# Two-layer adaptive-norm transformer block on one core: the last addition of x moved to GpSimd, ends of stages and the output projection rewritten

## The chip, the cores and the metric

The kernel runs on one core of one Trainium2 chip. The metric is device time in microseconds of one execution. Three executions of the kernel before took 2568.30, 2572.04 and 2572.55 us; the median is 2572.04 us. The execution that was profiled took 2576.07 us, and its profile spans 2574.3 us.

## The reference

`x` has 2 sequences of 2048 tokens, 256 wide, in float32. Both layers add a gated attention part and a gated feed-forward part. Cut to what matters:

```
mod = silu(c) @ wmod                      # sa, ca, ga, sb, cb, gb per sequence
h = layernorm(x)*(1+ca)+sa
x = x + ga * attention(h)                 # layer 0: 16 causal heads with rope; out @ W_o.T
h = layernorm(x)*(1+cb)+sb
x = x + gb * (h + expert[argmax(gate)](h))        # layer 0: top-1 of 8 experts, 256x256 each
h = layernorm(x)*(1+ca)+sa
x = x + ga * (silu-gated mix of 4 sequences(h) + h)   # layer 1
h = layernorm(x)*(1+cb)+sb
x = x + gb * (sum over the top 2 of 8 experts of w_e * FFN_e(rmsnorm(h)))
```

The output projection is `attention @ W_o.T`, and the last line's sum, gate and addition of `x` are the combination.

## The kernel before

The program is eight stages, one block of five instruction streams each: modulation, projections, attention, output projection, top-1 experts, layer 1 (mixing and routing), routed experts, combination. `k.x` (32 tiles of 128 tokens by 256) stays in SBUF throughout. Within a stage the engines are tied by semaphores alone, written out by hand; there is no scheduler. Each stage ends with a barrier of the five engines. At it every engine runs a DRAIN, GpSimd (POOL) too, and then waits for the others. Between blocks SyncE (SP) clears the semaphores of the stage that ended, one instruction each (line 2326 in `end_stage`), and only then comes to its own part of the next block; the other engines don't wait for the clearing.

GpSimd issues direct DMAs in modulation and attention and indirect ones (scatters) in layer 1 and the routed experts. In the other stages it has only arithmetic, or nothing.

Output projection: for each of 8 chunks of 512 tokens ScalarE copies `k.x` to `still`, TensorE turns it with 8 transposes into `p_t`, ScalarE copies that to `aT`, TensorE makes 8 products of 256 columns into `p_o`, VectorE multiplies by the gate (line 1036), adds the input (line 1040) and takes row statistics (line 250). `still`, `aT`, `p_t` and `p_o` have one buffer each. TensorE waits for the weights before its first transposes.

Top-1 experts: SP loads the expert weights at the stage's start. ScalarE rounds them (lines 1154, 1156), GpSimd subtracts to get the low parts (lines 1129, 1132), and ScalarE comes to the first tile's `hT` (line 1140) after its rounding. In layer 1 VectorE waits, before it centers its first rows, for the routing tables, the last of SP's twelve loads, to copy the token numbers (line 1829). At that stage's end SP writes zeros behind the last row of each expert, ten DMAs, eight of them with an address read from SBUF (lines 1395 and 1398).

Combination: for each of 8 chunks ScalarE scales the first expert's rows (line 2263), VectorE adds the second's (line 2272, four instructions), multiplies by the gate (line 2275) and adds `k.x` (line 2277); SP stores each chunk.

## Time and profile before

| | |
|---|---|
| median of 3 executions | 2572.04 us (2568.30 to 2572.55) |
| the profiled execution | 2576.07 us |
| its span | 2574.3 us |
| TensorE busy (matmul) | 2215.2 us (86%) |
| VectorE busy | 1698.4 us (66%) |
| ScalarE busy | 1275.8 us (50%) |
| GpSimd busy | 871.4 us (34%) |
| mean granted TensorE clock | 0.926 |

Shares of busy time are means over eight stages with different limits. An end of a stage is a point that all engines pass, so a microsecond gained before one is gained by all that follows, unless what follows waits for something else. Such ends are read from the timeline, and from the instructions recorded at the block's own line (its DRAINs and semaphore instructions).

### The profile page before, as it was taken

The page shows a single profiled execution, that of the slowest core. Times are in us where ns is not written, and L with a number is a line of the kernel's source. Part 1 is how long each engine was busy: PE and PEld are TensorE (multiplying, and loading weights), DVE is VectorE, ACT ScalarE, POOL GpSimd, SP SyncE. Part 2 cuts the span into 40 slices and gives each one's busy share as a digit, 9 for nine tenths or more (in the row PEclk, how much of TensorE's full clock was granted, in tenths as well). Part 3 has the DMA queues.
Part 4 walks back from the last instruction along what each step waited for, and adds up shares of the span by engine and source line. Part 5 has one row for each costly group of instructions (what it writes and reads, how often), then busy time and mean ns, then how long its engine had stood idle before and what let it go on. Part 6 is the DMA issues. An engine that isn't in the chain of part 4 may idle for free. (4 is left out here: it accounts for less than half of the span.)

```text
span 2574.3 us, 39299 instructions
## 1 busy us (share of the span) xinstructions
PE 2215.2 (86%) x12968; PEld 1404.0 (55%) x12968; DVE 1698.4 (66%) x2697; ACT 1275.8 (50%) x2451; POOL 871.4 (34%) x1055
## 2 busy tenths in 40 slices
PE   3886999999999999986799779972899999999991
PEld 1673233333333333325577546642788888888880
DVE  4784878778777878844688668863455555555555
ACT  1231477666767767773223244421455555555452
POOL 3344223221230311200655422444344434444340
PEclk8896799999999999998899889985999999999995
DMA  4359503150413400002000100013453433444326
GB/s 169 98 156 182 88 2 47 23 68 2 67 15 55 48 21 3 2 1 70 33 0 0 32 1 1 33 38 139 144 173 130 149 128 128 161 160 138 126 73 206
DMA packets 126575, 200.16 MB, mean 78 GB/s; under 512 B 13696, under 2 KB 98688, under 8 KB 124992
## 3 DMA queue, kind: packets, MB, share of 16 engines
q1 hardware_dynamic: 109696, 141.45, 16.6%
q0 software_dynamic: 15600, 52.25, 10.7%
q10 hardware_dynamic: 1104, 4.20, 1.2%
q8 instruction: 102, 1.67, 0.3%
q14 instruction: 73, 0.60, 0.1%
HBM read 150.97 MB, written 46.88 MB: 77 GB/s over the span
## 5 line engine op out<-in xcount | busy, mean ns | idle before, releaser
L905 DVE TENSOR_REDUCE tile_max<-p_m 128x2 f32<-128x1024 f32 (+3 forms) x640 | 651.4, 1060 | 150.1 <-PE p_m L767 78.7
L867 ACT ACTIVATE probs<-p_s 128x512 f32<-128x512 f32 (+3 forms) x1280 | 597.3, 534 | 247.9 <-PE p_s L776 243.0
L2061 PE MATMUL p_up<-f_xT,f_w 128*128 128x512 f32 (+1 forms) x2304 | 463.2, 350 | 8.2 <-POOL f_w L2224 8.2
L2061 PEld LDWEIGHTS p_up<-f_xT,f_w 128*128 128x128 f32 x2304 | 368.3, 189 | 58.8 <-issue 8.6
L714 POOL TENSOR_SCALAR_AFFINE_SELECT probs<-probs 128x128 f32<-128x128 f32 x512 | 145.7, 294 | 724.2 <-ACT probs L867 715.5
L763 PE MATMUL p_m<-ka,qa 96*128 96x512 bf16 (+3 forms) x1280 | 363.9, 367 | 29.5 <-PEq L330 17.4
L776 PE MATMUL p_s<-qa,ka 99*128 99x512 bf16 (+3 forms) x1280 | 353.8, 353 | 19.6 <-DMA qa<-max_scr 8.3
L2224 POOL TENSOR_TENSOR f_w<-f_raw,f_w 128x1024 fp32r<-128x1024 f32 x96 | 231.6, 2416 | 408.0 <-ACT f_w L2113 408.0
L790 PE MATMUL p_o<-probs,va 128*32 128x512 f32 (+3 forms) x2560 | 302.4, 544 | 0.3 <-POOL probs L714 0.3
L2076 PE MATMUL p_y<-f_w,f_hidden 128*128 128x256 f32 x1872 | 256.3, 283 | 28.9 <-DVE f_hidden L2178 14.6
L2076 PEld LDWEIGHTS p_y<-f_w,f_hidden 128*128 128x128 f32 x1872 | 237.7, 188 | 50.9 <-issue 31.7
L763 PEld LDWEIGHTS p_m<-ka,qa 96*128 96x128 bf16 x1280 | 111.7, 100 | 261.2 <-DVE tile_max L905 140.2
L2174 DVE SCALAR_TENSOR_TENSOR f_gate<-p_up,f_b,f_gate 128x512 f32<-128x512 f32 (+1 forms) x192 | 124.6, 649 | 194.0 <-ACT f_gate L2126 187.7
L776 PEld LDWEIGHTS p_s<-qa,ka 99*128 99x128 bf16 x1280 | 111.2, 98 | 228.3 <-ACT probs L867 139.7
L2178 DVE TENSOR_TENSOR f_hidden<-f_gate,f_hidden 128x512 fp32r<-128x512 f32 (+1 forms) x192 | 133.9, 698 | 118.7 <-ACT f_hidden L2131 114.0
L2126 ACT ACTIVATE f_gate<-p_up,f_b 128x512 f32<-128x512 f32 (+1 forms) x192 | 116.4, 606 | 172.2 <-PE p_up L2061 159.9
L1173 PE MATMUL p_e<-w_expert,c_hT 128*128 128x512 f32 x768 | 196.6, 406 | 0.0
L2131 ACT ACTIVATE f_hidden<-f_gate 128x512 fp32r<-128x512 f32 (+1 forms) x192 | 105.9, 552 | 159.5 <-DVE f_gate L2174 138.5
L1173 PEld LDWEIGHTS p_e<-w_expert,c_hT 128*128 128x128 f32 x768 | 141.4, 191 | 29.9
L2113 ACT ACTIVATE f_w<-f_raw 128x1024 fp32r<-128x1024 f32 x144 | 150.4, 1045 | 5.4 <-DMA f_raw<-in_W1b 3.6
L507 PE MATMUL p_qk<-hT,wqkv 128*128 128x512 f32 x384 | 99.3, 418 | 18.1 <-DVE rot L406 15.7
L1591 PE MATMUL p_uv<-l_xnT,w_uv 128*128 128x512 f32 x256 | 112.9, 598 | 0.0
(251 smaller groups left out, 2579.5 us busy)
## 6 DMA issues: line engine op xcount, KB each, us to landing
f_raw<-in_W1a SPq DMA_DIRECT2D x24, 1024.0 KB, 6.1
f_raw<-in_W1b SPq DMA_DIRECT2D x24, 1024.0 KB, 8.5
f_raw<-in_W SPq DMA_DIRECT2D x24, 1024.0 KB, 11.2
qk_scr<-parts SPq DMA_DIRECT2D x48, 256.0 KB, 2.5
qa<-qk_scr POOLq DMA_DIRECT2D x42, 256.0 KB, 15.4
ka<-qk_scr POOLq DMA_DIRECT2D x42, 256.0 KB, 17.2
v_scr<-wqkv_raw SPq DMA_DIRECT2D x32, 256.0 KB, 3.3
g_ys<-y_rows SPq DMA_DIRECT2D x16, 512.0 KB, 8.8
```

The lines of the kernel that those rows point to most:

```text
L714: last = nc.gpsimd.affine_select(block_, block_, pattern=[[1, P]], compare_op=ALU.is_ge, fill=0.0, base=0, channel_multiplier=-1)
L763: last = nc.tensor.matmul(p_m[:, at_bank, hh, 0:width], qa[buf][0:QROWS, hd, q0:q0 + P], ka[buf][0:QROWS, hd, bank * CH:bank * CH + width] ...
L776: nc.tensor.matmul(p_s[:, s_bank(x, buf), lo:CH], ka[buf][0:QROWS + SPLIT, h, j * P:(j + 1) * P], qa[buf][0:QROWS + SPLIT, h, c * CH + lo: ...
L790: last = nc.tensor.matmul(p_o[VW * h:VW * (h + 1), lo:CH], va[buf][:, j, VW * h:VW * (h + 1)], probs[:, (buf * UNITS + n) % NPROBS, h, lo: ...
L867: nc.scalar.activation(probs[:, (buf * UNITS + n) % NPROBS, h, lo:CH], p_s[:, s_bank(("exp", HG * n + h), buf), lo:CH], ACT.Exp, scale=DH ...
L905: nc.vector.tensor_reduce(out=tile_max[:, 2 * hp:2 * hp + 2, i, bank], in_=p_m[:, at_bank, :, 0:width], op=ALU.max, axis=AX.X).then_inc(ma ...
L1173: last = nc.tensor.matmul(out, hT[:, par, hp, kt, :], weights(wp, kt), start=(kt, wp, hp) == (0, HI, HI), stop=(kt, wp, hp) == (KT - 1, LO ...
L2061: last = nc.tensor.matmul(p_up[:, f % 2, ab, 0:size], w1[:, wh, ab * KT + kt, f * P:(f + 1) * P], xT[:, t % 2, xh, kt, 0:size], start=(kt, ...
L2076: last = nc.tensor.matmul(p_y[:, u, :], hidden[:, f % 2, hh, u * P:(u + 1) * P], w2[:, wh, f, :], start=(f, wh, hh) == (0, HI, HI) and u % ...
L2113: nc.scalar.activation(piece_part(q, HI), piece_raw(q, par), ACT.Copy).then_inc(w_high, 1)
L2178: nc.vector.tensor_tensor(hidden[:, f % 2, LO, 0:size], gate[:, f % 2, 0:size], hidden[:, f % 2, HI, 0:size], ALU.subtract).then_inc(hidde ...
L2224: nc.gpsimd.tensor_tensor(piece_part(q, LO), piece_raw(q, t % 2), piece_part(q, HI), ALU.subtract).then_inc(w1_ready, 1)
```

## The change

Six things change; attention's and the routed experts' inner loops, the projections and the steady part of the top-1 experts stay.

1. In the combination GpSimd adds `k.x` instead of VectorE.
2. Attention, layer 1 and the routed experts end without GpSimd's DRAIN.
3. SP clears the semaphores of the stage before after it has issued its first loads (in attention, before its first transfer).
4. The output projection is unrolled and has two buffers of `still`, `aT`, `p_t` and `p_o`. TensorE turns chunk i+1 before the products of chunk i, and turns chunk 0 before it waits for the weights.
5. The expert weights of the next stage are loaded, rounded (ScalarE) and subtracted (GpSimd) in the output projection.
6. In layer 1 the token numbers are copied when the first group chooses; and ScalarE's queue takes five of the ten zero writes.

```diff
-        with nc.Block() as block:                        # attention, layer 1, routed experts
+        with nc.Block(no_gpsimd_drain=True) as block:
...
 def output_projection(nc, a, k, ew):
             def _(sp):
                 sp.dma_start(w[:, :, :], a["woT"]...).then_inc(w_loaded, 16)
                 load(0)
                 load(1)
+                sp.dma_start(ew.raw_gate[:, :, :], ...).then_inc(e_loaded, 16)
+                sp.dma_start(ew.iota[:, :], a["iota8"]).then_inc(e_loaded, 16)
+                sp.dma_start(ew.raw[:, :, :], a["expertT"]...).then_inc(e_loaded, 16)
+                clear_last_stage(sp)
...
+            def _(pool):
+                pool.wait_ge(e_high, 1)
+                nc.gpsimd.tensor_tensor(ew.gate[:, LO, :, :], ew.raw_gate[:, :, :], ew.gate[:, HI, :, :],
+                                        ALU.subtract).then_inc(e_ready, 1)
+                for bank in range(BANKS):
+                    pool.wait_ge(e_high, bank + 2)
+                    nc.gpsimd.tensor_tensor(ew.bank(ew.w[:, LO, :, :], bank), ew.bank(ew.raw, bank), ew.bank(ew.w[:, HI, :, :], bank),
+                                            ALU.subtract).then_inc(e_ready, 1)
+                pool.wait_ge(e_ready, 1 + BANKS)
...
+                keep(0)                                  # ScalarE: keep copies k.x, copy takes p_t
+                keep(1)
+                for i in range(NCH):
+                    copy(i)
+                    if i + 2 < NCH:
+                        keep(i + 2)
+                    if i == NCH - BANKS - 1:
+                        act.wait_ge(e_loaded, 16 * E_LOADS)
+                        nc.scalar.activation(ew.gate[:, HI, :, :], ew.raw_gate[:, :, :], ACT.Copy).then_inc(e_high, 1)
+                    if NCH - BANKS - 1 <= i < NCH - 1:
+                        round_bank(i - (NCH - BANKS - 1))
...
+                turn(0)                                  # TensorE
+                pe.wait_ge(w_loaded, 16)
+                for i in range(NCH):
+                    if i + 1 < NCH:
+                        turn(i + 1)
                     pe.wait_ge(aT_ready, i + 1)
-                    if not first(i):
-                        pe.wait_ge(scaled, i)
+                    if i >= 2:
+                        pe.wait_ge(scaled, i - 1)
...
 def top1_experts(nc, a, k, ew):
-                act.wait_ge(loaded, 16 * LOADS)
-                nc.scalar.activation(gate[:, HI, :, :], raw_gate[:, :, :], ACT.Copy).then_inc(w_high, 1)
-                for bank in range(BANKS):
-                    nc.scalar.activation(bank_of(w, HI, bank), raw[:, :, bank * CH:(bank + 1) * CH], ACT.Copy).then_inc(w_high, 1)
                 round_hT(0, 0)
...
 def layer1(nc, a, k):
+                zero_tails(sp, range(E1 // 2), 0)
+                zero_tails(act, range(E1 // 2, E1), 1)
                     if g == 0:
                         dve.wait_ge(route_loaded, 16 * ROUTE_LOADS)
+                        c_own.add(nc.vector.tensor_copy(row_ids[:, :, 0], token_no))
...
-                dve.wait_ge(route_loaded, 16 * ROUTE_LOADS)
-                c_own.add(nc.vector.tensor_copy(row_ids[:, :, 0], token_no))
                 dve.wait_ge(rstd_all, 1)
...
 def combine(nc, a, k, out):
+                clear_last_stage(sp)                     # after the 16 loads
...
+            @block.gpsimd
+            def _(pool):
+                for i in range(NCH):
+                    pool.wait_ge(gated, i + 1)
+                    nc.gpsimd.tensor_tensor(res[:, rows_of(i), :], res[:, rows_of(i), :], k.x[:, rows_of(i), :], ALU.add).then_inc(done, 1)
...
                     nc.vector.tensor_tensor(rows, rows, k.mod(1, i // CPS, GB), ALU.mult).then_inc(gated, 1)
-                    dve.wait_ge(gated, i + 1)
-                    nc.vector.tensor_tensor(rows, rows, k.x[:, rows_of(i), :], ALU.add).then_inc(done, 1)
...
 def end_stage(nc):
-    for sem in Mem.of_stage:
-        nc.sync.sem_clear(sem)
+def clear_last_stage(sp):
+    for sem in Mem.cleared:
+        sp.sem_clear(sem)
```

TensorE at the end of attention and the start of the output projection, before (`o_pt` and `o_po` are the PSUM tiles of the transposes and of the products):

```order
L806 MATMUL p_m<-ident,o_sb 128x128 x3
L698 UNCONDITIONAL_BRANCH
L1007 UNCONDITIONAL_BRANCH [waits barrier_Pool_Activation_PE_DVE_SP_release]
L1013 MATMUL o_pt<-ident,o_still 128x128 [waits o_still_ready,o_w_loaded]
L1013 MATMUL o_pt<-ident,o_still 128x128 x7
L1021 MATMUL o_po<-wo,o_aT 128x256 [waits o_aT_ready]
L1021 MATMUL o_po<-wo,o_aT 128x256 x7
```

The same place after:

```order
L808 MATMUL p_m<-ident,o_sb 128x128 x3
L699 UNCONDITIONAL_BRANCH
L1059 UNCONDITIONAL_BRANCH [waits barrier_Pool_Activation_PE_DVE_SP_release]
L1067 MATMUL o_pt<-ident,o_still 128x128 [waits o_still_ready]
L1067 MATMUL o_pt<-ident,o_still 128x128 x7
L1067 MATMUL o_pt<-ident,o_still 128x128 [waits o_still_ready,o_w_loaded]
L1067 MATMUL o_pt<-ident,o_still 128x128 x7
L1081 MATMUL o_po<-wo,o_aT 128x256 [waits o_aT_ready]
L1081 MATMUL o_po<-wo,o_aT 128x256 x7
```

A second set of transposes now stands ahead of the first products, and the wait for the weights (`o_w_loaded`) stands one chunk later.

SP at the end of the routed experts and in the combination, before (`f_b` is a bias, `g_ys` the experts' rows, `g_res` the result; line 2326 is the clearing):

```order
L2032 DMA f_b<-in_b 128x256
L2007 UNCONDITIONAL_BRANCH
L2326 ISA [waits barrier_Pool_Activation_PE_DVE_SP_release]
L2326 ISA x22
L2245 UNCONDITIONAL_BRANCH
L2250 DMA g_ys<-y_rows 128x4x256 x16
```

and after (line 2370 is the clearing):

```order
L2063 DMA f_b<-in_b 128x256
L2038 UNCONDITIONAL_BRANCH
L2277 UNCONDITIONAL_BRANCH [waits barrier_Pool_Activation_PE_DVE_SP_release]
L2282 DMA g_ys<-y_rows 128x4x256 x16
L2370 ISA x23
```

The 23 clears moved from ahead of the 16 loads to behind them.

GpSimd from the end of attention to the first steps of the top-1 experts, before (`probs` belongs to attention, `c_h` to the first tiles of the top-1 experts):

```order
L714 AFFINE_SELECT probs<-probs 128x128 [waits probs_ready] x160
L698 UNCONDITIONAL_BRANCH
L1100 UNCONDITIONAL_BRANCH [waits barrier_Pool_Activation_PE_DVE_SP_gather]
L260 TENSOR_TENSOR rstd<-ve,neghalf 128x32 [waits ve_ready]
L1105 TENSOR_TENSOR c_h<-c_h,mods 128x256 [waits c_h_centered]
```

and after:

```order
L715 AFFINE_SELECT probs<-probs 128x128 [waits probs_ready] x160
L699 UNCONDITIONAL_BRANCH
L1020 UNCONDITIONAL_BRANCH [waits barrier_Pool_Activation_PE_DVE_SP_gather]
L1023 TENSOR_TENSOR w_gate<-c_raw_gate,w_gate 128x16 [waits o_e_high]
L1027 TENSOR_TENSOR w_expert<-c_raw,w_expert 128x2x512 [waits o_e_high] x4
L1001 UNCONDITIONAL_BRANCH [waits o_e_ready]
```

The five subtractions of the expert weights moved into the output projection, where GpSimd had nothing.

## Rows read from the trace of the kernel before

**Rows 1.** End of attention on VectorE, and the start of the output projection (timeline).

```profile
start us, us, engine line op out<-in xcount [idle before <-releaser]
1165.58 0.42 DVE L933 TENSOR_TENSOR x<-p_m,recip 128x256 f32<-128x256 f32 x1
1171.05 1.06 ACT L997 ACTIVATE o_still<-x 128x1024 f32<-128x1024 f32 x1 [6.65 <-PEq L698]
1172.09 0.43 SPq L984 DMA_DIRECT2D wo<-in_woT  x1
1174.99 1.97 PE L1013 MATMUL o_pt<-ident,o_still 128*128 128x128 f32 x8 [9.81 <-DMA wo<-in_woT]
1178.07 4.27 PE L1021 MATMUL o_po<-wo,o_aT 128*128 128x256 f32 x12 [1.11 <-ACT o_aT L1001]
```

**Rows 2.** GpSimd's DRAINs at three stage ends (ns min/median/max, start us).

```profile
L698 POOLq DRAIN  x1: 7972/7972/7972, 1162.8 to 1162.8; - x1
L1376 POOLq DRAIN  x1: 5382/5382/5382, 1782.6 to 1782.6; - x1
L2007 POOLq DRAIN  x1: 6417/6417/6417, 2523.8 to 2523.8; - x1
```

**Rows 3.** A steady chunk of the output projection, and its last statistics (timeline).

```profile
1196.61 3.32 PEld L1021 LDWEIGHTS o_po<-wo,o_aT 128*128 128x128 f32 x16 [1.35 <-ACT o_aT L1001]
1199.96 1.01 PEld L1013 LDWEIGHTS o_pt<-ident,o_still 128*128 128x128 f32 x8
1226.21 1.40 DVE L250 BATCH_NORM_STATS2 stats<-x  x4
```

**Rows 4.** Start of the top-1 experts (timeline).

```profile
1236.76 0.69 PE L1167 MATMUL c_pt<-ident,c_h 128*128 128x128 f32 x2 [13.60 <-POOL c_h L1107]
1241.28 0.36 ACT L1140 ACTIVATE c_hT<-c_pt 128x256 fp32r<-128x256 f32 x1
```

**Rows 5.** Start of layer 1 (timeline).

```profile
1468.54 5.44 POOL L1434 TENSOR_TENSOR rstd<-ve,neghalf 128x32 f32<-128x32 f32 x1 [3.31 <-DVE ve L243]
1479.42 0.20 DVE L1829 COPY xn_rows<-r_table 128x32 f32<-128x32 f32 x1 [10.94 <-DMA r_table<-in_tile_table]
```

**Rows 6.** End of layer 1, start of the routed experts (timeline).

```profile
1769.62 17.11 SPq L1398 DMA_DIRECT2D x_slots<-u_sb  x10
1785.38 0.41 DVE L1946 COPY weights<-r_pair_weights 128x16 f32<-128x16 f32 x4
1793.84 0.41 SPq L2016 DMA_DIRECT2D f_x<-x_slots  x1
```

**Rows 7.** SP's clears after layer 1 (instructions of a line, ns); combination's loads (timeline).

```profile
L2326 SPq EVENT_SEMAPHORE_RANGE_CLEAR  x42: 25/30/40, 1790.2 to 1793.0; - x42
...
2531.83 19.60 SPq L2250 DMA_DIRECT2D g_ys<-y_rows  x16
```

**Rows 8.** The combination: a load-paced ScalarE step, first and last VectorE work (timeline).

```profile
2540.59 1.71 ACT L2263 ACTIVATE g_res<-g_ys,weights 128x256 f32<-128x256 f32 x4 [1.31 <-DMA g_ys<-y_rows]
2538.12 1.68 DVE L2272 SCALAR_TENSOR_TENSOR g_res<-g_ys,weights,g_res 128x256 f32<-128x256 f32 x4 [19.60 <-ACT g_res L2263]
2569.80 1.23 DVE L2277 TENSOR_TENSOR g_res<-g_res,x 128x1024 f32<-128x1024 f32 x1
```

**Rows 9.** VectorE beside GpSimd's 128x1024 additions in layer 1 (timeline).

```profile
1490.57 3.39 DVE L1684 TENSOR_SCALAR l_h<-x,mean,rstd 128x256 f32<-128x256 f32 x4
1498.44 1.38 DVE L1684 TENSOR_SCALAR l_h<-x,mean,rstd 128x256 f32<-128x256 f32 x4
1644.69 4.65 POOL L1412 TENSOR_TENSOR l_h<-l_h,l_ob 128x1024 f32<-128x1024 f32 x2
1644.78 4.66 DVE L1673 TENSOR_TENSOR r_same<-l_logits,r_best 128x64 f32<-128x64 f32 x1
```

**Rows 10.** GpSimd's DMA issues by line: ns min/median/max, first and last start.

```profile
L281 POOL DMA_DIRECT2D ka<-qk_scr x42: 505/505/539, 234.4 to 880.3; - x42
L1429 POOL DMA_INDIRECT x_slots<-xn_rows,slots x64: 956/962/6556, 1613.8 to 1778.9; - x64
L2216 POOL DMA_INDIRECT y_rows<-f_y,f_y_to x78: 954/967/986, 1861.7 to 2520.5; - x78
```

More of the change, by code:

```diff
@@ L976, in output_projection, with rows_of @@
         scaled, x1_ready = m.sem("o_scaled"), m.sem("o_x1_ready")
+        e_loaded, e_high, e_ready = m.sem("o_e_loaded"), m.sem("o_e_high"), m.sem("o_e_ready")
+        E_LOADS = 3
+        def rows_of(i):
+            return slice(i * TPC, (i + 1) * TPC)
         with nc.Block() as block:
@@ L986, in _ @@
-                load(1, 1)
-                with sp.Fori(1, NCH // 2) as i:
-                    for par in range(2):
-                        sp.wait_ge(x1_ready, 2 * i + par - 1)
-                        load(2 * i + par, par)
+                load(0)
+                load(1)
+                sp.dma_start(ew.raw_gate[:, :, :], a["gateT"].rearrange("(k p) n -> p k n", p=P)).then_inc(e_loaded, 16)
+                sp.dma_start(ew.iota[:, :], a["iota8"]).then_inc(e_loaded, 16)
+                sp.dma_start(ew.raw[:, :, :], a["expertT"].rearrange("(k p) n -> p k n", p=P)).then_inc(e_loaded, 16)
@@ new lines, in _ @@
+                clear_last_stage(sp)
+                for i in range(2, NCH):
+                    sp.wait_ge(x1_ready, i - 1)
+                    load(i)
+                sp.wait_ge(e_loaded, 16 * E_LOADS)
+            @block.gpsimd
[8 more added lines that the diff above has]
+                pool.wait_ge(e_ready, 1 + BANKS)
@@ L1003, in _, with keep, copy @@
-                chunk(0)
-                with act.Fori(1, NCH) as i:
-                    chunk(i)
+                def keep(i):
+                    if i >= 2:
+                        act.wait_ge(turned, i - 1)
+                    nc.scalar.activation(still[:, i % 2, :, :], k.x[:, rows_of(i), :], ACT.Copy).then_inc(still_ready, 1)
+                def copy(i):
+                    act.wait_ge(turned, i + 1)
+                    if i >= 2:
+                        act.wait_ge(product, i - 1)
+                    nc.scalar.activation(aT[:, i % 2, :, :], p_t[:, i % 2, :, :], ACT.Copy).then_inc(aT_ready, 1)
@@ L1007, in _, with turn @@
             @block.tensor
             def _(pe):
-                def chunk(i):
+                def turn(i):
                     pe.wait_ge(still_ready, i + 1)
+                    if i >= 2:
+                        pe.wait_ge(aT_ready, i - 1)
                     for kt in range(KT):
                         for u in range(TPC):
-                            last = nc.tensor.transpose(p_t[:, kt, u * P:(u + 1) * P], still[:, u, kt * P:(kt + 1) * P],
+                            last = nc.tensor.transpose(p_t[:, i % 2, kt, u * P:(u + 1) * P], still[:, i % 2, u, kt * P:(kt + 1) * P],
@@ L1374, in p_logits, with zero_tails @@
             return p_l_last if j == 2 * LAST + 1 else p_l[:, j % 2, :, :]
-        with nc.Block() as block:
+        def zero_tails(engine, experts, part):
+            engine.wait_ge(tails_ready, 1)
+            engine.dma_start(k.x_slots[E1 * REGION + part * HT:E1 * REGION + (part + 1) * HT, :].rearrange("(p u) d -> p (u d)", p=P),
+                             zeros).then_inc(tails_zeroed, 16)
+            for e in experts:
+                at_row = engine.value_load(k.tails[0:1, e:e + 1], min_val=0, max_val=NSLOT - ST)
+                engine.dma_start(k.x_slots[bass.ds(at_row, HT), :].rearrange("(p u) d -> p (u d)", p=P), zeros).then_inc(tails_zeroed, 16)
+        with nc.Block(no_gpsimd_drain=True) as block:
             @block.sync
@@ L2005, in last_tile @@
             return t == NTILES - 1
-        with nc.Block() as block:
+        with nc.Block(no_gpsimd_drain=True) as block:
             @block.sync
@@ L2256, in _ @@
                 sp.wait_ge(stored, 16 * NCH)
+            @block.gpsimd
+            def _(pool):
+                for i in range(NCH):
+                    pool.wait_ge(gated, i + 1)
+                    nc.gpsimd.tensor_tensor(res[:, rows_of(i), :], res[:, rows_of(i), :], k.x[:, rows_of(i), :], ALU.add).then_inc(done, 1)
             @block.scalar
```

112 lines of the change are left out of this document (43 added, 69 removed).

## The prediction

> **What bounds the kernel now.** I read the page first. TensorE is busy 86% of the span, but the slices in which it falls to 0 to 7 tenths are the ends of stages and the last slice, and those are where the change acts. So I read, in order, the instructions recorded at each block's own line (who came last to each barrier), the timeline on both sides of each barrier, a steady chunk of the output projection, and the combination. The reader is to see five places where nothing useful happens, and one engine that sets the pace at the end.
>
> At the end of attention VectorE finishes at 1165.58 + 0.42 = 1166.0 us [rows 1], but ScalarE starts the next stage at 1171.05. The last to arrive is GpSimd: its DRAIN runs from 1162.8 for 7.97 us, to 1170.77 [rows 2]; passing the barrier takes the other 0.28 us. After the routed experts it is the same: a DRAIN of 6.42 us from 2523.8, then SP's clears, and the first load at 2531.83 [rows 2, 7]. After layer 1 a DRAIN of 5.38 us ends at 1788.0, but SP is later still: its ten zero writes take 17.11 us to issue, it passes the barrier just ahead of its first clear at 1790.2, clears until 1793.0 and issues the first load at 1793.84, while VectorE was done at 1785.79 [rows 2, 6, 7]. In the output projection a chunk is a chain in one buffer: the weights' loads of the products run from 1196.61 to 1199.96 and those of the transposes 1.01 us more, then TensorE waits 1.35 us for ScalarE's copy [rows 3]. In the combination ScalarE waits for each load (1.71 us of work and 1.31 of waiting, 3.02 per chunk [rows 8]), and VectorE, from 2538.12 to 2571.03, takes 32.9 us for 8 chunks, 4.11 each [rows 8]: VectorE is the bound there, the loads would be the next.
>
> **The change part by part**, against the profiled execution (2576.07 us, span 2574.3).
>
> *End of attention.* Without the DRAIN the barrier opens at 1166.0 + 0.28 = 1166.3. ScalarE's copy ends at 1167.3, the transposes and the second copy take what they took, 1178.07 - 1174.99 = 3.08 us [rows 1]; the second set of transposes stands ahead of the products and adds up to 1 us, so the products start at 1171.3. The weights are issued at 1166.4 and landed 2.90 us after their issue before (1172.09 to 1174.99 [rows 1]), so at 1169.3: not late. Before, the products started at 1178.07: -6.8 us.
>
> *Two buffers.* Before, from 1178.07 to the last statistics at 1227.61 [rows 1, 3]: 49.5 us. After, TensorE needs 3.35 + 1.05 = 4.40 us a chunk with no wait. VectorE needs three operations of 1.23, 1.23 and 1.40 us [rows 3, 8] and small gaps, some 3.95, and stays below that. First chunk 5 us (the slow one, [rows 1]: 4.27 for 12 of its 16 products), seven of 4.40, then 0.6 and 3.95 for VectorE: 40.3. That is -9.2 us. GpSimd's four new subtractions can hold VectorE's addition (below); most of that goes into VectorE's slack of 0.45 us a chunk, and I take +0.5 back. ScalarE has three operations of about 1.05 us a chunk in 4.40 and hides the rounding. Range of this part -6 to -10.
>
> *Start of the top-1 experts.* The transposes end at 1237.45, but ScalarE comes to their result at 1241.28 because it rounds weights until then [rows 4]. The rounding is gone: -3.8 us. What is late next is the chain through `rstd` and the transposes, which is already in that 1237.45.
>
> *Start of layer 1.* `rstd` is there at 1468.54 + 5.44 = 1473.98, yet VectorE stands until 1479.42 for the routing tables [rows 5]. The wait goes, a copy of 0.2 us comes back later: -5.3 us.
>
> *End of layer 1.* SP's tail is split in two queues, so that either issues five of ten writes in about half of 17.11 us, from 1769.6 to some 1778, and VectorE, done at 1785.79 [rows 6], becomes the last. Barrier at 1786.1, then the 0.84 us that SP took from its last clear to the first load (1793.0 to 1793.84 [rows 6, 7]): 1786.9 against 1793.84, -6.9 us. The 42 clears now stand after the loads of the second tile, where SP waits for its turn anyway.
>
> *End of the routed experts.* Barrier at 2523.8 + 0.3 and no clears ahead of the loads: 2524.1 against 2531.83, -7.7 us.
>
> The sum up to here: 6.8 + 8.7 + 3.8 + 5.3 + 6.9 + 7.7 = 39.2 us earlier.
>
> *GpSimd's addition in the combination.* VectorE loses 1.23 us of work a chunk, GpSimd gets an addition of 4.65 / 2 = 2.3 us by the layer 1 pair [rows 9], 2.4 taken. It would fit beside VectorE if the two ran side by side. In layer 1 they don't: a VectorE operation on 64 elements per row lasted 4.66 us because it started 0.09 us after the first of two such additions, and ended with the second [rows 9], and four others that take 1.38 us took 3.39 beside the pair's first [rows 9]. So one addition costs VectorE 3.39 - 1.38 = 2.0 to about 2.3 us. All that VectorE still does in the combination has both inputs in SBUF, like the first of these. I take 2.2. Then: 8 x 2.86 of VectorE's own, seven additions in its way at 2.2, the last with nothing beside it, 0.1 + 2.4: 22.9 + 15.4 + 2.5 = 40.8 us against 32.9, +7.9 (by 2.0 and 2.4: +6.5 and +9.3). The part that was moved to relieve VectorE makes its stage longer.
>
> The Trainium skill says more (SBUF — State Buffer, Who interferes with whom): a VectorE instruction with two SBUF inputs and a GpSimd instruction that reads SBUF share a read interface, and the second to issue blocks until the first is finished. By that rule every addition costs its whole length, seven times 2.4, and the stage is at the upper of my two values; these rows agree within 0.4 us an addition. It is the rule that speaks against moving work from the one engine to the other here.
>
> *Where the DRAINs go.* The one of attention took 7.97 us although its last DMA had been issued at 880.3 to 881 us, some 280 us before, and 160 GpSimd operations of attention lay between [rows 2, 10]. So it does not wait for transfers, and arithmetic on GpSimd does not work it off. Its length follows the number of DMAs since the last DRAIN: 5.38 us for 64, 6.42 for 78 [rows 2, 10], 0.084 and 0.082 us each. Leaving the instruction out then only defers the cost to the next DRAIN. For attention's that is the output projection's, which GpSimd reaches with its last subtraction, about chunk 6, some 12 us ahead of the stage's end: hidden, worth +0 (up to 8 if it were reached last). For layer 1's 64 and the routed experts' 78 it is the combination's, after the last addition: 142 x 0.083 = 11.8 us, where before only 2574.3 - 2571.03 = 3.3 us lay between the last addition and the end, the store. So +8.5 us. No trace shows a deferred DRAIN; the ends are 0 (it costs nothing if put off) and 8.5, and I take 8.5, since the attention row is just that case: late, and paid in full.
>
> Sum: -39.2 + 7.9 + 8.5 = -22.8 us; 2576.07 becomes 2553.3. The profiled execution lies 4.0 us over the median of the runs shown, 2572.04, so I predict 2549 for the median.
>
> **The rivals.**
> - *The DRAIN's cost isn't carried over*, or only the last stage's 78 DMAs (6.4 instead of 11.8, +3.1 over the store). For it: nothing shows two stages' DMAs in one DRAIN. Against it: attention's row. The time: 2549.2 - 8.5 = 2540.7, or 2543.8.
> - *The barriers don't open earlier*: the flag leaves the waiting somewhere else, in the next GpSimd instruction or in the barrier itself. Then attention gives back 4.8 us (1170.77 - 1166.0), layer 1 2.2 (1788.0 - 1785.8), the routed experts 6.4, and the combination's 8.5 doesn't arise: 2549.2 + 13.4 - 8.5 = 2554. Little speaks for it, since each engine's barrier step waits only for the others' signal.
> - *GpSimd adds beside VectorE*. Then the combination is paced by the loads: 7 x 3.02 + 2.9 + 2.4 = 26.4 us instead of 32.9, and the time is 2549.2 - 7.9 - 6.5 = 2535. Against it: all of rows 9.
> - *Slower than before: the scatters pay.* With no DRAIN since the output projection, GpSimd might have to clean up its finished DMAs inside the routed experts, at each scatter. A tile lasts (2523.8 - 1793.84) / 24 = 30.4 us; GpSimd works 4 x 2.3 for the subtractions and 3.25 scatters of 1.27 us (0.97 and a gap of 0.3) in it, which leaves 17 us, 5.2 for each scatter. Up to there it is hidden. If each scatter paid a whole DRAIN, 6.4 us, the stage would grow by 78 x 1.2 = 95 us, to some 2644 us; it turns into a loss over 0.2% from 0.36 us beyond the 5.2. Against it: 78 scatters stay within 954 and 986 ns, and attention's many direct DMAs within 505 and 539, with no clean-up in any [rows 10].
>
> **How the numbers follow.** The forecast 0.55, no or partial carrying 0.22, barriers unchanged 0.08, additions side by side 0.05, slower 0.04; the remaining 0.06 is for gains at stage starts that the next stage swallows (2555 to 2566). The likeliest case's own range, from the bounds of the addition's price and of the output projection, is 2544 to 2555. The range that should hold 8 in 10 reaches down to the uncarried DRAIN and up past the unchanged barriers: 2538 to 2558. A change below 0.2% (5.1 us) can't be told from none here. Every case but the last is faster by more than that: faster 0.94, same 0.02, slower 0.04.
>
> **What would show it.** In the profile after: ScalarE starts the output projection within 0.5 us of attention's last VectorE work; products begin there every 4.4 us; layer 1's first centering follows `rstd` at once; SP's first load of the routed experts comes about 1.1 us after VectorE's last copy. In the combination VectorE's four `g_res` operations that follow an addition take about 3.9 us instead of 1.7, a chunk lasts 5.1 us, and the last row of all is a GpSimd DRAIN near 11.8 us. I am wrong if that DRAIN is short, if the chunk lasts near 3 us, or if the subtractions in the output projection hold VectorE so that its chunks take over 5 us.

## The result, and the profile after

Four executions of the changed kernel took 2537.22 to 2539.70 us, median 2538.45; four of the kernel before, on the same chip, 2568.30 to 2572.55, median 2571.53 (the three shown first and one of 2571.02). The ratio is 0.9873, 95% interval 0.9856 to 0.9891. The forecast was 2549 with a range of 2538 to 2558: the time lies in the range, half a microsecond from its lower end, and outside the 2544 to 2555 of the likeliest case. From the median of 2572.04 it is 33.6 us, where 23.0 were forecast.

The profiled execution took 2537.22 us and spans 2535.5 us, 38.8 less than before. The barriers that end the stages, read in every profile from GpSimd's semaphore step at the block's line, give the length of each stage. The experiments stand beside for use below; every row is one profiled execution.

| us | to the end of projections | attention | output projection | top-1 | layer 1 | routed | combination |
|---|---|---|---|---|---|---|---|
| before | 232.8 | 938.1 | 56.9 | 239.4 | 322.8 | 740.4 | 43.8 |
| after | 232.2 | 929.9 | 42.4 | 235.1 | 311.1 | 731.2 | 53.5 |
| addition on VectorE | 230.9 | 930.7 | 42.9 | 235.3 | 311.2 | 731.7 | 42.6 |
| no last DRAIN | 232.0 | 930.5 | 43.0 | 235.5 | 311.2 | 731.8 | 50.1 |
| DRAIN after routed | 231.1 | 930.3 | 43.2 | 235.5 | 311.6 | 737.9 | 50.0 |
| before + GpSimd's addition | 232.0 | 932.9 | 56.8 | 239.6 | 322.4 | 739.8 | 51.2 |
| parts in PSUM | 232.4 | 933.5 | 42.3 | 235.1 | 310.1 | 732.1 | 38.1 |
| one buffer | 232.4 | 934.0 | 54.8 | 234.9 | 309.8 | 729.7 | 53.3 |
| clears first | 234.0 | 932.4 | 44.5 | 235.5 | 310.1 | 733.3 | 54.5 |
| zeros on SP | 232.8 | 935.8 | 42.9 | 235.4 | 311.0 | 732.1 | 53.2 |
| DRAINs back | 232.5 | 938.0 | 43.5 | 237.1 | 314.7 | 737.6 | 49.5 |
| longer chain | 232.4 | 935.8 | 43.0 | 235.4 | 310.8 | 738.3 | 50.1 |
| one new DMA | 232.3 | 931.0 | 43.1 | 235.6 | 311.3 | 731.5 | 53.0 |

End of attention and start of the output projection after, in the timeline (columns as in [rows 1], to which they answer).

```profile
1161.45 0.42 DVE L935 TENSOR_TENSOR x<-p_m,recip 128x256 f32<-128x256 f32 x1
1162.25 0.43 SPq L1008 DMA_DIRECT2D wo<-in_woT  x1
1162.26 2.00 ACT L1036 ACTIVATE o_still<-x 128x1024 f32<-128x1024 f32 x2 [1.98 <-PEq L699]
...
1163.37 3.62 PE L1067 MATMUL o_pt<-ident,o_still 128*128 128x128 f32 x16 [2.31 <-ACT o_still L1036]
...
1166.57 3.48 PEld L1081 LDWEIGHTS o_po<-wo,o_aT 128*128 128x128 f32 x16
...
1202.95 1.41 DVE L250 BATCH_NORM_STATS2 stats<-x 128x6 f32<-128x256 f32 x4
```

ScalarE starts 0.4 us behind VectorE's last work, where it was 5.05. Products start 4.70 us behind it, where it was 12.07, and from there to the last statistics it is 37.8 us, where it was 49.5 [rows 1, 3]. But VectorE itself is done 4.1 us sooner than before, in a stage whose loop the change doesn't touch. Two stretches of that loop, before and then after (busy time and count of PE, PEld, DVE, ACT, POOL; granted clock; DMA share; GB/s):

```profile
560.00:600.00 40.00, 37.99 (x244) 13.65 (x242) 26.86 (x36) 26.27 (x55) 4.56 (x16) 0.91 0.23 43
```

```profile
560.00:600.00 40.00, 39.19 (x269) 14.59 (x269) 30.67 (x41) 28.91 (x60) 4.54 (x16) 1.00 0.18 38
```

In this stretch TensorE was for a while at 1.2 instead of 2.4 GHz in the one execution and not in the other (a mean granted clock of 0.91 and of 1.00), and got 244 instead of 269 multiplications done. Such dips come in every profile here, most at changing places; attention without a DRAIN behind it lasts 929.9 to 935.8 us in the table. Added up in stretches of 20 us from 240 to 1140, the time that the clock withheld (one less the granted clock, times 20) is 35.4 us before and 31.8 after; it is 30.4 in the kernel with a DRAIN after the routed experts, whose attention lasts 930.3, and 37.4 in the one with all zero writes on SP, where it lasts 935.8. So 3.6 of the 4.1 us are the clock's dips and not a gain; the execution profiled before lay 4.0 us over its median.

GpSimd's DRAINs after (ns min/median/max, start), which answer to [rows 2]:

```profile
L1001 POOLq DRAIN  x1: 7492/7492/7492, 1193.3 to 1193.3; - x1
...
L2276 POOLq DRAIN  x1: 8829/8829/8829, 2526.4 to 2526.4; - x1
...
L2276 SPq DRAIN  x1: 7/7/7, 2531.9 to 2531.9; - x1
```

Attention's DRAIN is paid in the output projection, 7.49 us, and ends at 1200.8, ahead of VectorE: hidden. The last DRAIN starts while the last addition runs (below) and outlasts it by 6.4 us; SP had its stores landed at 2531.8, so 3.4 us of it are on the path, not 8.5. Here one of the prediction's own signs fails: the DRAIN is not near 11.8 us.

A chunk of the output projection beside a subtraction of the expert weights, the first steps of top-1 and of layer 1 ([rows 3, 4, 5]):

```profile
1178.79 2.37 POOL L1027 TENSOR_TENSOR w_expert<-c_raw,w_expert 128x1024 fp32r<-128x1024 f32 x1 [0.71 <-ACT w_expert L1045]
...
1179.15 1.22 DVE L1089 TENSOR_TENSOR o_gated<-o_po,mods 128x1024 f32<-128x1024 f32 x1 [0.34 <-PE o_po L1081]
1179.71 3.32 PEld L1081 LDWEIGHTS o_po<-wo,o_aT 128*128 128x128 f32 x16
...
1180.48 1.76 DVE L1093 TENSOR_TENSOR x<-o_gated,o_xin 128x1024 f32<-128x1024 f32 x1
...
1184.04 3.32 PEld L1081 LDWEIGHTS o_po<-wo,o_aT 128*128 128x128 f32 x16
...
1213.49 0.69 PE L1195 MATMUL c_pt<-ident,c_h 128*128 128x128 f32 x2 [13.61 <-POOL c_h L1147]
1214.22 0.38 ACT L1172 ACTIVATE c_hT<-c_pt 128x256 fp32r<-128x256 f32 x1 [20.18 <-PE c_pt L1195]
...
1440.92 5.44 POOL L1465 TENSOR_TENSOR rstd<-ve,neghalf 128x32 f32<-128x32 f32 x1 [3.31 <-DVE ve L243]
...
1446.40 1.38 DVE L1716 TENSOR_SCALAR l_h<-x,mean,rstd 128x256 f32<-128x256 f32 x4 [5.53 <-POOL rstd L1465]
```

Products come every 4.33 us. VectorE's addition, both inputs in SBUF, is held until the subtraction ends (1.76 for 1.23 us); its multiplication, which reads PSUM, is not, although it lies wholly beside the subtraction. ScalarE and VectorE start the next two stages as soon as their inputs are there.

The end of layer 1 and the combination ([rows 6, 7, 8]), and with them who came last to layer 1's barrier (ns min/median/max, first and last start):

```profile
1745.45 0.96 POOL L1460 DMA_INDIRECT x_slots<-xn_rows,slots  x1 [0.30 <-issue]
...
1747.60 0.40 DVE L1977 COPY weights<-r_pair_weights 128x16 f32<-128x16 f32 x4
1751.55 0.42 SPq L2047 DMA_DIRECT2D f_x<-x_slots  x1
...
L1412 DVEq DRAIN  x1: 431/431/431, 1747.6 to 1747.6; - x1
L1412 SPq DRAIN  x1: 7/7/7, 1748.7 to 1748.7; - x1
L1412 POOLq EVENT_SEMAPHORE  x2: 17/17/17, 1750.6 to 1750.7; - x2
...
2482.03 19.85 SPq L2282 DMA_DIRECT2D g_ys<-y_rows  x16
...
2488.75 1.68 DVE L2311 SCALAR_TENSOR_TENSOR g_res<-g_ys,weights,g_res 128x256 f32<-128x256 f32 x4 [12.25 <-ACT g_res L2302]
...
2496.76 3.75 DVE L2311 SCALAR_TENSOR_TENSOR g_res<-g_ys,weights,g_res 128x256 f32<-128x256 f32 x4
2496.92 2.52 POOL L2295 TENSOR_TENSOR g_res<-g_res,x 128x1024 f32<-128x1024 f32 x1 [2.81 <-DVE g_res L2314]
...
2526.47 2.34 POOL L2295 TENSOR_TENSOR g_res<-g_res,x 128x1024 f32<-128x1024 f32 x1 [2.41 <-DVE g_res L2314]
```

VectorE is done at 1748.0, but SP's first load of the routed experts comes 3.55 us later and not 1.1: a second sign that fails. The last at the barrier is GpSimd, also without its DRAIN: its last scatter is issued at 1746.4, and it waits until 1750.6 for its scatters to land (a semaphore wait in the kernel).

VectorE's four `g_res` operations take 3.75 us beside an addition, 1.68 alone. From its first work to the end of the last addition it is 40.06 us, where it was 32.9.

### The profile page after: what moved, and what is told of

Read it like the earlier page. It is cut to its first block and busy times, and to the rows that moved or that the text cites. A ratio compares the mean times of both kernels' runs of the same rounds, so it can differ in the third digit from the quotient of the medians.

```text
span 2535.5 us, 39140 instructions
## 1 busy us (share of the span) xinstructions
PE 2208.5 (87%) x12968; PEld 1402.7 (55%) x12968; DVE 1703.5 (67%) x2689; ACT 1274.9 (50%) x2451; POOL 889.7 (35%) x1063
## 3 DMA queue, kind: packets, MB, share of 16 engines
q0 software_dynamic: 15600, 52.25, 10.9%
## 5 line engine op out<-in xcount | busy, mean ns | idle before, releaser
L869 ACT ACTIVATE probs<-p_s 128x512 f32<-128x512 f32 (+3 forms) x1280 | 597.0, 535 | 244.4 <-PE p_s L778 239.6
L765 PE MATMUL p_m<-ka,qa 96*128 96x512 bf16 (+3 forms) x1280 | 363.8, 367 | 29.1 <-PEq L330 17.2
```

The source lines that it names most:

```text
L765: last = nc.tensor.matmul(p_m[:, at_bank, hh, 0:width], qa[buf][0:QROWS, hd, q0:q0 + P], ka[buf][0:QROWS, hd, bank * CH:bank * CH + width] ...
L869: nc.scalar.activation(probs[:, (buf * UNITS + n) % NPROBS, h, lo:CH], p_s[:, s_bank(("exp", HG * n + h), buf), lo:CH], ACT.Exp, scale=DH ...
```

## The experiments

The spread of a kernel's executions is some ±4 us, as large as single terms, so where a term is small it is read from its stage in the table, and the median stands beside. The ratios are to the kernel before on the same chip, whose median was 2571.36 to 2573.70 us on the three chips that ran the experiments.

No run takes back the move of the expert weights (part 5) or of the token numbers (part 6). Their worth stands on the rows shown above.

**The addition back on VectorE.**

```diff
-            @block.gpsimd                            # combination: its additions
                     nc.vector.tensor_tensor(rows, rows, k.mod(1, i // CPS, GB), ALU.mult).then_inc(gated, 1)
+                    dve.wait_ge(gated, i + 1)
+                    nc.vector.tensor_tensor(rows, rows, k.x[:, rows_of(i), :], ALU.add).then_inc(done, 1)
```

> The changed kernel with one part undone: the last addition of x in the combination is VectorE's again, GpSimd has nothing to do there. Theory (while GpSimd adds, it holds VectorE's four additions of g_res: 3.75 us for four instead of about 1.7; the DRAIN at the program's end belongs to the scatters of the routed experts): a chunk of the combination takes 4.1 us instead of 4.93, the stage from VectorE's first to its last work 32.9 us instead of 40.1, and GpSimd's DRAIN stands at the stage's start, 6.4 us long, hidden. The span ends 42.5 us (43.9 less 1.4 of clears) after the barrier at 2482.0: 2524.5 against 2535.5, so about 11 us less than the changed kernel, median near 2527.5, ratio to before 0.983. Rival 1 (the four additions last 3.75 us for another reason, such as the loads): chunk stays at 4.9 us plus VectorE's own addition or is unchanged, time 2535 or more. Rival 2 (the DRAIN covers layer 1's 64 scatters too): its length is 8.8 (if it ran beside the last addition in the changed kernel) or 11.8 us.

Measured: median 2529.86 us (five, 2527.08 to 2533.14), ratio 0.9842 (0.9829 to 0.9856); the stage 42.6 instead of 53.5 us. VectorE's rows in the timeline, and the DRAIN's:

```profile
2501.42 1.67 DVE L2305 SCALAR_TENSOR_TENSOR g_res<-g_ys,weights,g_res 128x256 f32<-128x256 f32 x4
2503.12 1.22 DVE L2308 TENSOR_TENSOR g_res<-g_res,mods 128x1024 f32<-128x1024 f32 x1
2504.38 1.22 DVE L2310 TENSOR_TENSOR g_res<-g_res,x 128x1024 f32<-128x1024 f32 x1
2505.53 1.67 DVE L2305 SCALAR_TENSOR_TENSOR g_res<-g_ys,weights,g_res 128x256 f32<-128x256 f32 x4
```

```profile
L2276 POOLq DRAIN  x1: 6431/6431/6431, 2482.8 to 2482.8; - x1
```

The chunk is 4.11 us again, and with nothing ahead of it the DRAIN is 6.43 us: that of 78 scatters, not of 142. The theory holds, both rivals fall. By the stage, the addition on GpSimd costs the change 10.9 us: 7.1 by holding VectorE, 3.4 by the DRAIN that it pushes to the end, the rest between the first load and the first work. By the medians it is 8.6.

**The kernel before, with that addition alone.** The diff is the reverse of the one above, in the kernel before.

> The kernel before, with only the combination's last addition of x moved to GpSimd. Theory (each addition holds VectorE about 2.0 us and saves it 1.23): chunk 4.9 instead of 4.11 us, four g_res additions 3.75 us, stage 7 us longer, and no DRAIN of length at the end, since the one after the routed experts has done its work (0.05 us there): median 2571.5 + 7.2 = 2578.7, ratio 1.003. Rival (the two engines work side by side when loads come as in the kernel before, and the changed kernel's longer stage comes from its clears or its DRAIN): chunk 3.0 to 4.1 us, median 2565 to 2571.

Measured: median 2580.39 us (eight), ratio 1.0034 (1.0024 to 1.0044); the stage 51.2 instead of 43.8 us. The addition makes its stage 7.4 us longer by itself, against 7.2 expected; the medians differ by 9.0. This profile is also a second one of the old end of layer 1, and there it differs from [rows 6]:

```profile
1763.47 9.99 SPq L1398 DMA_DIRECT2D x_slots<-u_sb  x10
...
1774.62 0.41 DVE L1946 COPY weights<-r_pair_weights 128x16 f32<-128x16 f32 x4
...
1787.45 0.41 SPq L2016 DMA_DIRECT2D f_x<-x_slots  x1
```

```profile
L1376 POOLq DRAIN  x1: 5382/5382/5382, 1778.2 to 1778.2; - x1
```

The ten writes take 10.0 us, not 17.1. The barrier waits for GpSimd's DRAIN (to 1783.6), not for SP.

**No DRAIN at the end.**

```diff
-        with nc.Block() as block:                    # combination
+        with nc.Block(no_gpsimd_drain=True) as block:
```

> The changed kernel, and the combination too ends without GpSimd's DRAIN. Theory (the last DRAIN of 8.83 us, 6.4 of it behind the last addition, stands on the path by 3.4 us over the store): no DRAIN at the end, the span ends about 3.4 us sooner, at 2532, median near 2535. Rival (whatever was put off is paid at the end of the program in any case, in another instruction or in the time after the span): median 2538 as in the changed kernel.

Measured: median 2535.13 us (four, 2529.82 to 2539.95), ratio 0.9855 (0.9837 to 0.9874); the stage 50.1 instead of 53.5 us, -3.4 as expected. The executions of the two kernels overlap, so the medians alone (3.3 us apart) would not show it; but the stage is 53.0 to 53.5 us in the four profiles that end with this DRAIN of 8.8 us and have their clears behind the loads, and 50.1 here. Nor is it paid behind the span: from the span to the device time it is 1.7 us in both.

**A DRAIN after the routed experts.** That block's flag is taken away, attention's and layer 1's stay.

> The changed kernel with GpSimd's DRAIN at the end of the routed experts restored, while attention and layer 1 stay without it. Theory A (a DRAIN deals only with the DMAs of the stage that ends): 6.4 us there for 78 scatters, as in the kernel before, and the DRAIN at the program's end is 2.4 us (the last addition alone). Theory B (what layer 1's DRAIN would have done is carried over, 0.083 us for each of 142): 11.8 us. Theory C (142 carried at a lower price, 8.8 us in all as in the changed kernel's last DRAIN): 8.8 us. The boundary costs its DRAIN in full and the program's end gives 3.4 us back, so against the changed kernel: A +3.0, B +8.4, C +5.4 us.

Measured: median 2540.81 us, ratio 0.9881 (0.9866 to 0.9896). The two DRAINs:

```profile
L2038 POOLq DRAIN  x1: 6439/6439/6439, 2483.0 to 2483.0; - x1
```

```profile
L2276 POOLq DRAIN  x1: 2447/2447/2447, 2533.9 to 2533.9; - x1
```

Theory A: what layer 1's DRAIN would have done is not in it (2.45 us at the end is the last addition alone). The stage grows by 6.7 us and the last gives 3.5 back, +3.2 against +3.0 expected.

**A longer chain without a DRAIN.** The flag in attention, the output projection, top-1 and layer 1, and a DRAIN after the routed experts.

> The changed kernel with GpSimd's DRAIN left out in attention, the output projection, the top-1 experts and layer 1, and restored after the routed experts: nothing cleans up between attention's 91 DMAs, layer 1's 64 and the routed experts' 78. Theory Own (a DRAIN deals with the DMAs of the last stage that had any): 6.4 us after the routed experts. Theory Sum (all of them): 233 x 0.082 = 19.2 us. Theory Pair (attention's part survives because it was carried over a stage before): 6.4 + 7.5 = 13.9 us. If Own holds, the question is where attention's 7.5 us were paid: in an instruction of layer 1, or never.

Measured, one execution: 2547.65 us (clock dips in attention, 935.8 us). The DRAIN:

```profile
L2038 POOLq DRAIN  x1: 6435/6435/6435, 2489.2 to 2489.2; - x1
```

This is what Own expected. Nor were attention's 7.5 us paid elsewhere: layer 1 and the routed experts last 310.8 and 738.3 us, 311.6 and 737.9 in the run before, where attention's DRAIN had been paid. In layer 1 one scatter, the thirtieth, takes 6.56 us, but it does so in every kernel, also behind DRAINs, and the smallest, the middle and the largest of the 64 are the same (956, 962, 6561 ns; [rows 10]: 956, 962, 6556).

**One new DMA behind attention's.**

```diff
-                sp.dma_start(ew.iota[:, :], a["iota8"]).then_inc(e_loaded, 16)
...
+                pool.dma_start(ew.iota[:, :], a["iota8"]).then_inc(i_loaded, 16)     # first on GpSimd
```

> The changed kernel, with the small load of iota_e in the output projection issued by GpSimd instead of SP, at the stage's start. So attention's 91 DMAs, whose DRAIN was left out, are followed by one new DMA before the next DRAIN. Theory Stage (a DRAIN deals only with the DMAs issued since the stage before ended): the output projection's DRAIN is 0.1 us. Theory Debt (what was put off stays until a DRAIN, whatever comes between): 7.6 us. Theory Last-N (the DRAIN's length follows a number of the newest DMAs that stays constant or is bounded): 7.5 us. The stage is hidden either way, no change in time expected.

Measured, one execution: 2539.66 us. The output projection's DRAIN:

```profile
L1002 POOLq DRAIN  x1: 7565/7565/7565, 1195.2 to 1195.2; - x1
```

One new DMA doesn't wipe out what was put off (7.57 against 7.49 us), so Stage falls, and with it Own's wording: the last stage that had any DMA is here the output projection, with one. Debt fits here, but 6.4 us after 233 DMAs above is against it, and against Last-N too, which couldn't be shorter there than here.

**All three DRAINs back.**

> The changed kernel with GpSimd's DRAIN restored at the ends of attention, layer 1 and the routed experts. Theory (each was on the path in full once SP's clears and zero writes are out of the way, and the last stage's is deferred to the end where 3.4 us of it show): attention's boundary +4.7 us, layer 1's +5.4, the routed experts' +6.4, the program's end -3.4: +13 us, median 2551.5. Rival (the prediction's reading of layer 1, where SP and VectorE are the last and the DRAIN is worth 2.2 us at most): layer 1's stage grows by 2 to 3 us only, +10 us.

Measured: median 2555.65 us (four, 2548.74 to 2556.69), ratio 0.9932 (0.9911 to 0.9953). By stage: attention's barrier 4.8 us behind VectorE instead of 0.2, +4.6; layer 1 +3.6; routed experts +6.4; combination -4.0. That is +10.6 and nearer the rival's 10 than the theory's 13, since layer 1 grew by less than its DRAIN's 5.3. The median is 17.2 us higher. What the other 6.6 are is not shown; in the profile attention is 3.5 us longer up to VectorE's end, the output projection 1.1 and top-1 2.0.

**One buffer.** `i % 2` becomes 0 in the four tiles, and the waits are for the chunk before.

```diff
-                turn(0)
...
-                    if i + 1 < NCH:
-                        turn(i + 1)
+                    turn(i)
...
                     pe.wait_ge(aT_ready, i + 1)
-                    if i >= 2:
-                        pe.wait_ge(scaled, i - 1)
+                    if i >= 1:
+                        pe.wait_ge(scaled, i)
```

> The changed kernel with one buffer each of o_still, o_aT, o_pt and o_po in the output projection (the kernel before's chain of keep, transposes, copy, products; the weights are still waited for behind the first transposes, and the expert weights' rounding stays here). Theory (the two buffers bring most of the stage's gain): chunk 5.7 us instead of 4.33, the span from the first product to the last statistics 47.5 instead of 37.8 us, median 2538.5 + 10 = 2548.5. Rival (most of the stage's gain is that TensorE's clock is back at full speed sooner, or that the input loads come earlier): chunk below 5 us, median under 2543.

Measured: median 2551.11 us (four), ratio 0.9907 (0.9889 to 0.9925); the stage 54.8 instead of 42.4 us. The first two chunks, and the clock there and in the changed kernel:

```profile
1170.77 5.94 PEld L1075 LDWEIGHTS o_po<-wo,o_aT 128*128 128x128 f32 x16 [1.58 <-issue]
...
1179.09 3.32 PEld L1075 LDWEIGHTS o_po<-wo,o_aT 128*128 128x128 f32 x16 [1.35 <-ACT o_aT L1042]
...
1184.80 3.32 PEld L1075 LDWEIGHTS o_po<-wo,o_aT 128*128 128x128 f32 x16 [1.35 <-ACT o_aT L1042]
```

```profile
1171.00:1175.00 4.00, 4.00 (x10) 3.16 (x11) 0.00 (x0) 0.60 (x1) 0.00 (x0) 0.50 1.07 399
```

```profile
1167.00:1171.00 4.00, 4.00 (x23) 3.54 (x23) 0.51 (x1) 2.14 (x3) 0.00 (x0) 1.00 1.07 363
```

A chunk is 5.71 us instead of 4.33: 7 x 1.38 = 9.7 us. The other 2.5 us are the first chunk's: with one set of transposes and a wait ahead of the products, TensorE does them at 1.2 GHz (0.50) and takes 5.94 us; with two sets and no pause it is at 2.4 GHz by then and takes 3.48. The theory's 10 us are there, and the rival's clock adds 2.5 to them; that the clock is most of the gain, as the rival had it, is false.

**Clears ahead of the stages.** `end_stage` clears again, `clear_last_stage` does nothing.

> The changed kernel with SP's clears of the last stage's semaphores ahead of each stage again. Theory (each clear costs SP 0.067 us and the first loads wait for them where nothing else is late): the routed experts' first load comes 2.8 us later (42 clears), the combination's first load 1.5 us later (23), and the output projection's wo about 1 us later, hidden behind the first transposes and copy; median 2538.5 + 4.3 = 2542.8. Rival (other work hides the clears everywhere): no change, 2538.5.

Measured: median 2545.87 us (four), ratio 0.9885 (0.9867 to 0.9902). By stage: output projection +2.1, top-1 +0.4, layer 1 -1.0, routed experts +2.1, combination +1.0, 4.6 in all, against 4.3 expected. The median is 7.4 us higher, of which 2.2 are this chip's (the kernel before took 2573.70 on it). The size by stage was right, the place was not: I had called `wo` hidden, but issued 1.2 us behind the barrier (1167.57) instead of 0.1 it holds up the second transposes, whose queue place is behind the wait for it, and TensorE comes to the first products at a lower clock (4.23 instead of 3.48 us).

**Ten zero writes on SP.**

> The changed kernel with all ten zero writes at the end of layer 1 in SP's queue, as before. Theory N (the 17.1 us that they took in the profile of before belong to that one execution: in another profile of the same code they took 9.7 us, from 1763.5 to 1773.2, and VectorE's tail 12.9 instead of 17.6 us): they are issued within 10 us of 1735.3, GpSimd stays the last at the barrier, no change, median 2538.5 within 1. Theory P (the prediction's reading: ten in one queue take 17.1 us): SP is last, at 1752.4 and the landing of 4 us more, the barrier opens at 1757 instead of 1750.7, median 2544.

Measured: median 2540.74 us (four, 2534.99 to 2545.08), ratio 0.9862 (0.9844 to 0.9880); layer 1 311.0 us, as with two queues.

```profile
1743.84 8.90 SPq L1432 DMA_DIRECT2D x_slots<-u_sb  x8
1752.78 1.09 SPq L1434 DMA_DIRECT2D x_slots<-u_sb  x2
```

This is what theory N expected: the ten take 10.0 us, and the median is the changed kernel's but for the 2.2 us of this chip. SP, with its writes landed, comes to the barrier at 1757.7, GpSimd at 1757.9, so one queue is just fast enough. Splitting the writes brought nothing here; 17.11 us was one execution's.

**Parts in PSUM.** The unheld multiplication in the output projection suggested it.

```diff
+        part = m.ps("g_part", [P, 2, TPC, 2 * D])    # half of each row used
...
-        with nc.Block() as block:
+        with nc.Block(no_gpsimd_drain=True) as block:
...
+                    if i >= 2:
+                        act.wait_ge(gated, i - 1)
...
-                        nc.scalar.activation(res[:, t, :], ys[:, 0, t, :], ACT.Copy, ...
+                        nc.scalar.activation(part[:, i % 2, t % TPC, 0:D], ys[:, 0, t, :], ACT.Copy, ...
...
-                        nc.vector.scalar_tensor_tensor(out=res[:, t, :], ..., in1=res[:, t, :], ...
+                        nc.vector.scalar_tensor_tensor(out=part[:, i % 2, t % TPC, 0:D], ..., in1=part[:, i % 2, t % TPC, 0:D], ...
...
-                    nc.vector.tensor_tensor(rows, rows, k.mod(1, i // CPS, GB), ALU.mult)
+                    nc.vector.tensor_tensor(rows, part[:, i % 2, :, 0:D], k.mod(1, i // CPS, GB), ALU.mult)
```

> The changed kernel, with what lies between ScalarE and VectorE in the combination kept in PSUM: ScalarE's scaled rows and VectorE's sum go to a PSUM tile with two buffers, VectorE's gate multiplication reads it and writes g_res to SBUF, GpSimd still adds x, and the combination ends without GpSimd's DRAIN. Each of VectorE's instructions there then has one input in PSUM and one in SBUF. Theory A (GpSimd's additions hold only VectorE instructions with both inputs in SBUF: in the changed kernel's output projection the multiplication that reads o_po took 1.21 to 1.22 us beside GpSimd's subtractions, and the addition with both inputs in SBUF 1.56 to 1.76 instead of 1.23): four g_res additions take 1.7 us beside GpSimd, VectorE and GpSimd work side by side, a chunk is paced by its loads at 3.0 us; from VectorE's first work to the last addition 26.4 us instead of 40.1, then 3.3 to the end: span 2518.5, median near 2521.5, ratio 0.980. Rival B (GpSimd holds VectorE wherever both work, or PSUM is slower for VectorE): four additions 3.8 us, chunk 4.9, median 2535 as without the DRAIN.

Measured: median 2525.46 us (five, 2523.45 to 2527.97), ratio 0.9811 (0.9797 to 0.9825), the fastest of all.

```profile
2491.97 1.68 DVE L2314 SCALAR_TENSOR_TENSOR g_part<-g_ys,weights,g_part 128x256 f32<-128x256 f32 x4 [12.02 <-ACT g_part L2305]
...
2500.49 1.67 ACT L2305 ACTIVATE g_part<-g_ys,weights 128x256 f32<-128x256 f32 x4 [1.34 <-DMA g_ys<-y_rows]
2501.00 1.68 DVE L2314 SCALAR_TENSOR_TENSOR g_part<-g_ys,weights,g_part 128x256 f32<-128x256 f32 x4
2501.01 2.35 POOL L2296 TENSOR_TENSOR g_res<-g_res,x 128x1024 f32<-128x1024 f32 x1 [0.66 <-DVE g_res L2317]
2502.72 1.22 DVE L2317 TENSOR_TENSOR g_res<-g_part,mods 128x1024 f32<-128x1024 f32 x1
2503.50 1.67 ACT L2305 ACTIVATE g_part<-g_ys,weights 128x256 f32<-128x256 f32 x4 [1.34 <-DMA g_ys<-y_rows]
```

Beside GpSimd's addition the four operations now take 1.68 us, the chunk is 3.0 us, and what it waits for is the load. Against the kernel that also has no last DRAIN the stage is 38.1 instead of 50.1 us: -12.0 for the place of one tile. The expected 2521.5 us were missed by 4: attention lasts 3.6 us longer than in the changed kernel, and 5.3 instead of 3.3 us lie behind the last addition, where the last store takes at least 4.8 us to land (2.9 in the kernel before).

The Trainium skill has the rule (SBUF — State Buffer, Who interferes with whom): a VectorE instruction with at most one SBUF input, outside the modes in which it uses both of its pairs of ports, doesn't contend with GpSimd. These rows agree, 1.68 us beside GpSimd's addition and 1.68 in the first chunk, ahead of any. The condition on the modes matters: in [rows 9] the four `TENSOR_SCALAR` of `l_h` read one tensor from SBUF, and were held all the same, 3.39 instead of 1.38 us.

## Why the prediction came out as it did

Term by term, from the two profiles:

| | predicted | measured |
|---|---|---|
| VectorE's end of attention | 0 | -4.1 (clock dips) |
| from there to the first products | -6.8 | -7.4 |
| to the last statistics | -8.7 | -11.7 |
| top-1, to layer 1's `rstd` | -3.8 | -4.4 |
| start of layer 1 | -5.3 | -5.5 |
| end of layer 1 | -6.9 | -9.1 |
| routed experts to the combination's first load | -7.7 | -7.5 |
| to VectorE's first work there | 0 | +0.4 |
| the combination, serialised | +7.9 | +7.1 |
| behind the last addition | +8.5 | +3.4 |
| sum | -22.8 | -38.8 |

The 4.1 us of the first line were allowed for in another shape, as the 4.0 us by which the profiled execution lay over its median. The other 11.9 us are errors, and all large ones have one sign, so the time came near the range's end and the range held with little to spare.

- *The deferred DRAIN*, 5.1 us, is the step that failed, by the prediction's own signs as well. "For layer 1's 64 and the routed experts' 78 it is the combination's: 142 x 0.083 = 11.8 us" generalised from a length that fitted a count in three rows. Attention's was carried, in full and hidden, as said (7.49 us; of the 7.97 before, 0.5 lie beside its last select). Layer 1's was not: the DRAIN is 6.4 us after 142 DMAs (by itself in two kernels, 6.43 and 6.44, behind the last addition in the changed one, 6.42) and after 233 (6.44), as it is after 78. This was the rival of partial carrying (2543.8), which shared a chance of 0.22 with that of none.
- *The two buffers*, 3.0 us, right in mechanism and too small: -11.7 lies outside the -6 to -10 given for this part. The first chunk was priced at 5 us by the slow row of before, where TensorE, which had stood still, was at 1.2 GHz (a granted clock of 0.50 until 1179 us); the second set of transposes, which I counted only as a cost of 1 us, also wakes the clock (3.48 us). The last chunk has no transposes ahead of its products (1.0 us), and the hold of VectorE's addition cost nothing.
- *The end of layer 1*, 2.2 us. The sum leaned on SP's 17.11 us and VectorE's end at 1785.79, which belong to that one execution: two other profiles show 10.0 us for the same ten writes, and the split of the queue did nothing. What the runs show there is GpSimd's DRAIN, 3.6 us of the stage when it is put back, and the clears, 2.1 us; no run takes back the other 3.4. The forecast gave the DRAIN away as 2.2 us, credited SP instead, and made VectorE the last, where it is GpSimd with its scatters in flight: it came near by chance.
- *GpSimd beside VectorE* was right: 3.75 us against 3.9, a chunk of 4.93 against 5.1, +7.1 against +7.9, and the price of the addition by itself is shown twice.
- The ends of attention and of the routed experts, top-1 and the start of layer 1 were right within 0.6 us each. The clears' price is known as a whole (4.6 us by stage), not barrier by barrier.

What stays open: what sets a GpSimd DRAIN's length. It is 5.4, 6.4 and 7.5 us for 64, 78 and 91 DMAs of the last stage that had many, is kept over a stage with none or one, and is not added over stages with many. Nor is it a price by the piece alone. In the kernel before, the first stage has two DMAs of GpSimd, of 2 MB each, and ends with the following DRAIN. It is off the path, since the barrier opens only at 45.5 us:

```profile
L140 POOLq DRAIN  x1: 21322/21322/21322, 1.8 to 1.8; - x1
```

It ends at 23.1 us. The second of the two DMAs is issued at 2.7, and the longer of the two landings takes 20.3 us, which makes 23.0; in the changed kernel the same two ends are 22.7 and 22.5. So here the DRAIN lasts until the transfers have landed. The prediction's "it does not wait for transfers" holds for attention, where they had long landed, and not in general.

Nor is it known why the thirtieth scatter of layer 1 takes 6.56 us in every kernel.

## What to carry to other kernels

Before work is moved from VectorE to GpSimd, look at what VectorE does meanwhile. Its operations on two tensors waited out GpSimd's instruction when both lay in SBUF, and didn't wait when one lay in PSUM; a `TENSOR_SCALAR` on one SBUF tensor waited too. Moving a tile to PSUM was worth more than the moved addition. A span of a single profile that decides a term (17.11 us for ten issues, with others' work stretched beside it) deserves a second look at how one instruction of the kind usually lasts. A stage's first products are priced by what TensorE did just before them, so work that fills its pause can pay twice.

## What the runs showed that was not expected

A DRAIN left out is paid in full in one place (7.49 us) and vanishes in another. The granted clock dips for some microseconds in attention in every profiled execution, mostly at places that change; that stage lasts 929.9 to 935.8 us in profiles of the same loop, and the longest are those with most clock withheld. That this makes the whole spread of this kernel's time is likely and not shown.
